# A mixer's decays clamped on ScalarE and its y gated on VectorE

## What is computed

```
h = layernorm(x) * (1 + ca) + sa
z, xBC, dt = split(h @ W_in.T)            # 1024, 1280, 16 columns
dt = softplus(dt + dt_bias)
xBC = silu(causal_conv4(xBC) + b_conv)    # X (16 heads of 64), B, C (128 each)
a = dt * -exp(A_log);  cs = cumsum(a) in a chunk
L[l, s, head] = exp(cs[l] - cs[s]) for s <= l, else 0
Y_diag = (C B^T * L) X;  Y_off = C state * exp(cs)
y = (Y_diag + Y_off + Dp * X) * silu(z)
y = y * rsqrt(mean(y*y) + 1e-5) * norm_w
x = x + ga * (y @ W_out.T)
```

## Time and profile before

| | |
|---|---|
| median of 3 runs | 1739.21 us (1736.09 to 1740.42) |
| the profiled execution's span | 1740.9 us, mean granted clock 0.938 |
| TensorE busy | 1569.5 us, 90% |
| VectorE busy | 1248.8 us, 72% |
| ScalarE busy | 627.0 us, 36% |
| GpSimd busy | 492.0 us, 28% |
| L889, the subtraction and clamp, VectorE | 512 instructions, 101.7 us |
| L543, L547, L549, the gating, GpSimd | 32 each, 105.6, 58.9 and 28.6 us |
| L689, the exponential, ScalarE | 64 instructions, 62.1 us |

### The profile page before, as it was taken

The page is one execution under the profiler, slowest core; times in us unless marked ns, Lnnn a source line. Parts: engine busy times, 40 slices in busy tenths (PEclk is TensorE's granted clock), DMA queues, the critical chain, the costliest instruction groups (busy, mean ns, idle before and its releaser), DMA issues. The chain is left out here.

```text
span 1740.9 us, 26906 instructions
## 1 busy us (share of the span) xinstructions
PE 1569.5 (90%) x8289; PEld 1276.2 (73%) x8289; DVE 1248.8 (72%) x2460; ACT 627.0 (36%) x1208; POOL 492.0 (28%) x440
## 2 busy tenths in 40 slices
PE   5989889988988898989988999875899999999998
PEld 5977777767767777767777777753688888888887
DVE  3779998888888988988988889853546445544543
ACT  3345445444554454434544444430211111201200
POOL 1323423433334233433342333433011111111111
PEclk9799999998999999989998999986899999999999
DMA  8312212121121111211221121104320120120110
GB/s 259 126 42 76 98 46 74 68 79 73 61 84 67 42 73 67 79 73 37 87 83 49 73 67 67 74 31 144 146 73 7 67 73 12 60 72 18 54 49 26
DMA packets 61377, 124.25 MB, mean 71 GB/s; under 512 B 13296, under 2 KB 15984, under 8 KB 56816
## 3 DMA queue, kind: packets, MB, share of 16 engines
q1 hardware_dynamic: 55632, 114.68, 18.9%
q10 hardware_dynamic: 5664, 8.65, 1.4%
HBM read 97.62 MB, written 25.69 MB: 71 GB/s over the span
## 5 line engine op out<-in xcount | busy, mean ns | idle before, releaser
L819 DVE SCALAR_TENSOR_TENSOR xBC<-conv_in,wconv,xBC 128x256 f32<-128x256 f32 x480 | 300.0, 629 | 12.7 <-ACT xBC L616 1.3
L1398 ACT ACTIVATE silu_gate<-bank,sgate 128x512 f32<-128x512 f32 x88 | 60.7, 689 | 383.4 <-PE bank L1517 383.4
L1183 PE MATMUL bank<-X,B_rows 128*128 128x512 f32 x128 | 90.8, 799 | 92.9 <-DVE state L955 88.7
L1452 DVE SCALAR_TENSOR_TENSOR hidden<-bank,sup,silu_gate 128x512 f32<-128x512 f32 x88 | 66.0, 750 | 145.8 <-PE bank L1517 145.8
L615 ACT ACTIVATE conv_in<-bank 128x256 f32<-128x256 f32 x160 | 61.5, 385 | 255.6 <-PE bank L1086 255.6
L1171 PEld LDWEIGHTS bank<-X,decay 128*128 128x128 f32 x1024 | 123.6, 195 | 30.8 <-issue 23.7
L1517 PE MATMUL bank<-ff_h_high,W_gate 128*128 128x512 f32 x352 | 141.5, 402 | 2.4 <-DVE ff_h_low L1440 2.4
L1171 PE MATMUL bank<-X,decay 128*128 128x64 f32 x1024 | 127.0, 278 | 16.4 <-DVE X_D L948 16.4
L1517 PE MATMUL bank<-ff_h_low,W_gate 128*128 128x512 f32 x352 | 140.1, 398 | 0.0
L1549 PE MATMUL bank<-W_down,hidden_high 128*128 128x512 f32 x352 | 139.5, 396 | 0.0
L1549 PE MATMUL bank<-W_down,hidden_low 128*128 128x512 f32 x352 | 139.5, 396 | 0.0
(11 more groups left out here) (170 smaller groups left out, 3493.2 us busy)
## 6 DMA issues: line engine op xcount, KB each, us to landing
decay<-sums_scratch SPq DMA_DIRECT2D x32, 1024.0 KB, 4.7
wq_rows<-wqT SPq DMA_DIRECT2D x33, 256.0 KB, 4.0
widened_scratch<-wq_rows SPq DMA_DIRECT2D x33, 256.0 KB, 2.0
x_tile<-x SPq DMA_DIRECT2D x32, 256.0 KB, 2.8
x_resid<-x SPq DMA_DIRECT2D x32, 256.0 KB, 2.7
x_scratch<-x_resid SPq DMA_DIRECT2D x32, 256.0 KB, 2.0
ff_x_tile<-x_scratch SPq DMA_DIRECT2D x32, 256.0 KB, 3.6
ff_x_resid<-x_scratch SPq DMA_DIRECT2D x32, 256.0 KB, 4.0
```

What stands on the lines that cost most here:

```text
L819: nc.vector.scalar_tensor_tensor(A.xc[b][:, m, :], A.raw[:, m, j:j + SC], A.wconv[:, m, j:j + 1], A.xc[b][:, m, :], ALU.mult, ALU.add).the ...
L1183: nc.tensor.matmul(state[:, 0:W], A.Btok[:], A.X[:, f * W:(f + 1) * W], start=True, stop=True).then_inc(state_done, 1)
L1398: nc.scalar.activation(B.sg[m % 2][:], gates[m % 2][:], ACT.Silu, scale=T.sgate[:, m:m + 1]) \
L1452: nc.vector.scalar_tensor_tensor(B.hid[m % 2][:], ups[m % 2][:], T.sup[:, m:m + 1], B.sg[m % 2][:], ALU.mult, ALU.mult).then_inc(hid_step, 1)
```

## The change

`diff` goes from VectorE. In its place ScalarE has `falls(u, c)`: 16 Relu activations of 128x128 with scale -1 and a per-partition bias (the column of `sums`), so relu(s - L), which is minus the clamped difference; `exp_decay` takes the exponential with scale -1. `falls(.,0)` stands behind `evac_ln` and ahead of `widen`, `falls(.,1)` behind `exp_sums` and ahead of the four `exp_decay`. `gate` goes from GpSimd to VectorE: `gate(0)` behind `conv(1)` and ahead of `read_state(0,0)`, `gate(1)` behind `decay_X(1)` and ahead of the two `norm`. One semaphore, `gate_z`, is new.

```diff
--- before.py
+++ after.py
@@ -354,11 +354,11 @@
             sem(s) for s in ("silu_done", "siluq_done", "e3_done", "edt_done", "decay_done", "sq_done"))
         stats_step, normed, split, conv_step, softplus_step, sums_step = (
             sem(s) for s in ("stats_step", "normed", "split", "conv_step", "softplus_step", "sums_step"))
-        tail_step, diff_done, G_masked, M_done, Xdec_done = (
-            sem(s) for s in ("tail_step", "diff_done", "G_masked", "M_done", "Xdec_done"))
+        tail_step, fall_done, G_masked, M_done, Xdec_done = (
+            sem(s) for s in ("tail_step", "fall_done", "G_masked", "M_done", "Xdec_done"))
         yoff_read, ydiag_read, S_step = sem("yoff_read"), sem("ydiag_read"), sem("S_step")
-        rstd_step, XD_done, y_summed, gated, rs_step, out_step = (
-            sem(s) for s in ("rstd_step", "XD_done", "y_summed", "gated", "rs_step", "out_step"))
+        rstd_step, XD_done, y_summed, gate_z, gated, rs_step, out_step = (
+            sem(s) for s in ("rstd_step", "XD_done", "y_summed", "gate_z", "gated", "rs_step", "out_step"))
 
         accs, tps = A.psum[0:2], A.psum[2:4]
         small, yoff, ydiag, state = A.psum[4:8]
@@ -536,18 +536,6 @@
                                         A.X[:].rearrange("p (h d) -> p h d", h=H),
                                         A.Drow[:].unsqueeze(2).broadcast_to([P, H, HD]), ALU.mult).then_inc(XD_done, 1)
 
-            def gate(n, u, b, c):
-
-                wait(pool, yoff_read, u, 2 * NC, 2 * c + 2)
-                wait(pool, ydiag_read, u, 2 * NC, 2 * c + 2)
-                nc.gpsimd.tensor_tensor(A.yt[:], A.yt[:], A.XD[:], ALU.add).then_inc(y_summed, 1)
-                wait(pool, y_summed, u, NC, c + 1)
-
-                a_wait(pool, a_emptied, u, ("z", 2 * c + 1), 1)
-                nc.gpsimd.tensor_tensor(A.yt[:, 0:Z], A.yt[:, 0:Z], A.siluz[:, c, :], ALU.mult)
-                wait(pool, siluq_done, u, 1, 1)
-                nc.gpsimd.tensor_tensor(A.yt[:, Z:], A.yt[:, Z:], A.zdt[1 - b][:, c, 0:ZQ], ALU.mult).then_inc(gated, 1)
-
             def inv_rms(n, u, c):
 
                 if u != 0:
@@ -571,14 +559,12 @@
                 own, bef, nxt = has_own(n), has_before(n), has_next(n)
                 if bef:
                     times_D(n, u, 0)
-                    gate(n, u, b, 0)
                     inv_rms(n, u, 0)
                     times_D(n, u, 1)
                 if nxt:
                     rstd(after(n))
                 if bef:
                     residual(n, u, b, 0)
-                    gate(n, u, b, 1)
                     inv_rms(n, u, 1)
                     residual(n, u, b, 1)
 
@@ -683,10 +669,19 @@
                 wait(act, yoff_read, u, 2 * NC, 0)
                 nc.scalar.activation(A.e3[:], A.s3[:], ACT.Exp).then_inc(e3_done, 1)
 
+            def falls(u, c):
+
+                wait(act, cs_in[c], u, 16, 16)
+                wait(act, sums_step, u, 3, 3)
+                for h in range(H):
+                    x = A.L[c][:, h, :]
+                    last = nc.scalar.activation(x, x, ACT.Relu, bias=A.s3[:, c * H + h:c * H + h + 1], scale=-1.0)
+                last.then_inc(fall_done, 1)
+
             def exp_decay(u, c, f):
-                wait(act, diff_done, u, 2 * NC, 2 * c + f + 1)
+                wait(act, fall_done, u, NC, c + 1)
                 x = A.L[c][:, f * HH:(f + 1) * HH, :]
-                nc.scalar.activation(x, x, ACT.Exp).then_inc(decay_done, 1)
+                nc.scalar.activation(x, x, ACT.Exp, scale=-1.0).then_inc(decay_done, 1)
 
             def exp_dt(n):
                 wait(act, softplus_step, n, SP_STEPS, 2)
@@ -767,10 +762,12 @@
                 if nxt:
                     evac_ln(after(n), 1 - b, n)
                 if own:
+                    falls(n, 0)
                     widen(n, 1)
                     silu_tile(n, b, 8)
                     silu_tile(n, b, 9)
                     exp_sums(n)
+                    falls(n, 1)
                     exp_decay(n, 0, 0)
                     exp_decay(n, 0, 1)
                     exp_decay(n, 1, 0)
@@ -872,23 +869,12 @@
 
                 wait(dve, e3_done, n, 1, 0)
                 wait(dve, cs_out, n, 16, 0)
-                wait(dve, diff_done, n, 2 * NC, 0)
+                wait(dve, fall_done, n, NC, 0)
                 nc.vector.tensor_copy(A.s3[:, 0:2 * NC * H], small[:, 0:2 * NC * H]).then_inc(sums_step, 1)
                 wait(dve, sums_step, n, 3, 1)
                 nc.vector.tensor_tensor(A.s3[:, 2 * NC * H:3 * NC * H], A.s3[:, NC * H:2 * NC * H],
                                         A.s3[:, 0:NC * H], ALU.subtract).then_inc(sums_step, 1)
                 nc.vector.tensor_copy(A.csT[:], small[0:NC * H, 2 * P:3 * P]).then_inc(sums_step, 1)
-
-            def diff(u, c, f):
-
-                if f == 0:
-
-                    wait(dve, cs_in[c], u, 16, 16)
-                    wait(dve, sums_step, u, 3, 3)
-                for h in range(f * HH, (f + 1) * HH):
-                    last = nc.vector.tensor_scalar(A.L[c][:, h, :], A.L[c][:, h, :], A.s3[:, c * H + h:c * H + h + 1],
-                                                   0.0, ALU.subtract, ALU.min)
-                last.then_inc(diff_done, 1)
 
             def mask_G(u):
                 wait(dve, G_done, u, 1, 1)
@@ -948,6 +934,19 @@
                 nc.vector.tensor_tensor(A.XD[:, f * W:(f + 1) * W], ydiag[:, 0:W], A.XD[:, f * W:(f + 1) * W],
                                         ALU.add).then_inc(ydiag_read, 1)
 
+            def gate(n, u, b, c):
+
+                wait(dve, yoff_read, u, 2 * NC, 2 * c + 2)
+                wait(dve, ydiag_read, u, 2 * NC, 2 * c + 2)
+                nc.vector.tensor_tensor(A.yt[:], A.yt[:], A.XD[:], ALU.add).then_inc(y_summed, 1)
+                wait(dve, y_summed, u, NC, c + 1)
+
+                a_wait(dve, a_emptied, u, ("z", 2 * c + 1), 1)
+                nc.vector.tensor_tensor(A.yt[:, 0:Z], A.yt[:, 0:Z], A.siluz[:, c, :], ALU.mult).then_inc(gate_z, 1)
+                wait(dve, siluq_done, u, 1, 1)
+                nc.vector.tensor_tensor(A.yt[:, Z:], A.yt[:, Z:], A.zdt[1 - b][:, c, 0:ZQ], ALU.mult).then_inc(gated, 1)
+                wait(dve, gate_z, u, NC, c + 1)
+
             def read_state(u, b, c, f):
                 wait(dve, state_done, u, 2 * NC, 2 * c + f + 1)
                 wait(dve, S_step, u, 4 * NC, 4 * c + 2)
@@ -1003,6 +1002,7 @@
                 if own:
                     conv(n, b, 1)
                 if bef:
+                    gate(n, u, b, 0)
                     read_state(u, b, 0, 0)
                 if own:
                     conv(n, b, 2)
@@ -1033,6 +1033,7 @@
                     read_yoff(n, u, b, 1, 1)
                     read_ydiag(u, 1, 1)
                     decay_X(n, u, 1)
+                    gate(n, u, b, 1)
                 if nxt:
                     norm(after(n), n, 0)
                     norm(after(n), n, 1)
@@ -1050,11 +1051,6 @@
                     tails(n, b)
                 if n == 0:
                     setup.vector_turn0(dve, 1)
-                if own:
-                    diff(n, 0, 0)
-                    diff(n, 0, 1)
-                    diff(n, 1, 0)
-                    diff(n, 1, 1)
                 if nxt:
                     split_h(after(n), n, 0)
                     split_h(after(n), n, 1)
```

## The result

The changed kernel takes 1782.76 us in the median of 4 runs (1780.53 to 1783.04); the kernel before, run beside it, 1737.65 us (4 runs). The ratio is 1.0255, 95% interval 1.0228 to 1.0282: slower by 2.6%, where 4.6% was forecast. The profiled span is 1781.0 us, 40 us more than before's 1740.9.

What follows compares the result with a forecast made beforehand. TensorE and VectorE were taken as near full, TensorE stalling on VectorE's read_state. Fifteen turns of 7.7 less 2.2 us make +82, loop branches -7, last turn +6: +81, so 1820 us, range 1782 to 1855.

Steps and rivals of the forecast that it cites:

- likeliest case: The whole kernel slows to 1820 us because the Relus delay TensorE; chance 0.73, own range 1790 to 1850 us.
- ScalarE's chain: ScalarE's list from evac_ln to scale_out(.,1): 32 Relus at 0.30 us each make it 9.7 us longer.
- Rival (a): Relus on ScalarE are cheaper, 0.22 us each: 41 us less, 1780 us; chance 0.11.
- Rival (c): Relu on ScalarE needs its own table, adding up to four loads a turn: +82 us, 1902 us; chance 0.04.
- project_zdt(.,1): TensorE's product at the turn's edge waits for scale_out's bank: 8.7 us late, after some 7 us idle.
- dt_first: VectorE, first half of a turn: its first instruction, held up by POOL's times_D, takes 1.89 us instead of 0.18.
- VectorE's relief: Without GpSimd's gate beside them, conv(1) returns 3.9 us, norms and conv(7) 4.0; each gate costs VectorE 2.5.
- the clock's term: Behind the shrunken states(1,1) stall, TensorE's clock may stay up, returning 1.4 us; half counted.
- second half: Turn's part up to states(1,1): the stall shrinks by 1.5 us; with half the clock's gain, -2.2 us.
- Rival (d): The Relus hide in half-busy ScalarE and VectorE's relief decides: 1695 us, down to 1655; chance 0.05.
- first half: Turn's part up to states(0,1): late project_zdt(.,1) and VectorE's list make that product start 7.7 us later.
- The ends: Last turn, where nothing covers the Relus but VectorE was already slow: +6 us.

Runs made afterwards that it cites:

- gate_only: The kernel before with the gate alone moved to VectorE, the subtraction staying on VectorE: 1644.83 us, ratio 0.9472.
- falls_only: The kernel before with the Relus alone moved to ScalarE, the gate staying on GpSimd: 1857.59 us, ratio 1.0690.
- pool_gate_tiny: The kernel before with the gate's three GpSimd instructions narrowed to 16 columns, the other columns left out: 1591.45 us, ratio 0.9159.

## Why the prediction was half right

The direction, the waits, their places and the engines were as forecast; the size was twice the measured one. Forecast +81 us of span, measured +40. The median of 1782.76 stands at the lower end of the range (1782 to 1855) and outside the likeliest case's own (1790 to 1850). Point by point:

- *ScalarE's chain* was forecast 9.7 us longer and is 9.33 longer; the Relus were sized at 0.30 us apart and are 0.292. Rival (a), 1780 us through Relus of 0.22, names nearly the measured time and is wrong: the Relus are as dear as I took them. Rival (c) is out by the trace, which has no further loads (35 in both kernels); the trace agrees with what the page "ScalarE: Activation LUTs" of the Trainium skill states of relu in its section "Table sets: the hidden batching unit".
- *`project_zdt(.,1)` late by 8.7 us, 7 us idle:* idle 6.6 us. The stretch from the G products to it grew by 6.94, and they themselves come 1.4 later (forecast 1.4, within the 8.7): 8.3 together.
- *`dt_first`:* I took 1.89 us for its first instruction, it takes 1.03; the low-clock stretch ahead of it was 1.3 us longer than at full speed (forecast 1.1). The cheaper instruction returned nothing to the turn, as `read_ydiag(0,0)` then waited 0.80 us for TensorE.
- *VectorE's relief:* 3.9 us at `conv(1)` forecast and measured; 4.0 at the norms and `conv(7)`, measured 3.6 + 0.5; a gate at 2.5 us, measured 2.5.
- *The step that failed* is the clock's term. In the second half it says "if the clock then stays up, 1.4 more come back. I count half", 0.7 us a turn for one of the two stretches, and for the other, behind `states(0,1)`, nothing, though the same sum has that stall shrink from 3.11 us to about 1 (TensorE free at 610.3, the state at 611.3). Both stretches stayed at the upper level in every turn of the loop, and they returned 3.7 us a turn: 2.18 behind `states(0,1)` and 1.50 behind `states(1,1)`. The 3.0 us that were missing make 45 us in 15 turns. Rival (d) priced both stretches in full, but only for the case in which the falls hide.
- *The pair of turns.* Over the two turns of a loop's pass the four stretches changed, on average, by +6.95 (edge), -1.36 (first half, forecast -1.0 and -0.75 for the branch), -3.78 (second half: -1.60 the stall, forecast -1.5, and -2.18 the clock) and -0.11 (+1.38 for the G products' wait, -1.50 the clock): +1.70 us a turn where +4.75 was forecast. Without the clock it is 5.4 against a forecast 5.45. That this fits so well is partly luck: the edge was 0.4 too dear, and the first half returned 0.4 less than forecast.
- *The ends:* +6 forecast for the last turn. 15 periods of 1.9 us explain 29 of the 40 us; 4 lie ahead of the first G mask, and some 7 behind the last. The turns were forecast at +75, so they were 46 us too dear and the ends 5 too cheap, which gives the 41.

So the mechanism was right and one term was mis-sized, the clock's share. It had rows for stalls of 3 us (0.50 and 0.58 behind them) and none for a stall of 1.4, and the half that I took for one of them was a guess.

## What to carry to other kernels

Work isn't moved to an engine but to a place in its list. ScalarE had half its time free and its Relus still cost 118 us where they stood in the one stretch that TensorE waits for; half of them moved into gaps gave 74 us back. Ask of each long GpSimd instruction what VectorE does beside it: three of them a chunk cost 143 us here, and TensorE hardly waited for them once. And price a stall with the slow stretch behind it, and also when it only shrinks.

## What the runs showed of the hardware that I had not expected

- A shorter wait can return more than its length, through the clock. Behind waits of 1.25 to 1.5 us (kernel after) and 1.7 (`gate_only`) TensorE stayed at 2.4 GHz, behind those of about 3 us it mostly fell to 1.2 for some 3 us. The length alone doesn't decide. In `falls_only` the second stall of every other turn in the loop had 2.98 to 3.02 us idle before it, and the work behind it ran at 1.00, as in the first two lines here; in the kernel before a stall of 1.83 us had slow work behind it, as in the last two. What decides between them stays open.

```profile
624.50 0.70 PE L1178 MATMUL bank<-X,B_rows 128*128 128x512 f32 x1 [2.98 <-DVE state L955]
```

```profile
624.50:628.00 3.50, 3.50 (x18) 2.65 (x19) 3.05 (x7) 0.97 (x2) 0.18 (x1) 1.00 0.00 0
```

```profile
815.08 1.25 PE L1183 MATMUL bank<-X,B_rows 128*128 128x512 f32 x2 [1.83 <-DVE state L955]
```

```profile
815.00:820.00 5.00, 4.92 (x23) 4.31 (x24) 4.52 (x18) 1.19 (x2) 0.00 (x0) 0.66 0.00 0
```

- `norm`, with a single tensor as input, was held up by GpSimd's tensor_tensor as much as the two-input convs: 2.1 us a piece in the kernel before, 0.54 in `pool_gate_tiny`. The Trainium skill, page "SBUF — State Buffer", section "SBUF: two separate sides", has it that a port pair goes to VectorE or to GpSimd for a whole instruction, and that a one-input instruction needs it only in VectorE's faster modes. The trace fits the first, as the two norms took 4.62 us beside `gate(1)` and 1.00 without it, but doesn't show the port itself; for the second there is only that `norm` takes 0.54 us for 512 columns where a tensor_tensor takes 0.68, and no run here tells the mode itself.
